# Norms of a state-space mixer: squares as the stationary operand, sums with time on the partitions

## The reference, cut to what matters

```python
proj = einsum('btd,od->bto', x, W_in)           # gate, value, and 2 step parameters a head
value = silu(conv(value_raw))
dt = clip(softplus(params[..., 0] + dt_bias), DT_MIN, DT_MAX)
kd = K_MAX * sigmoid(params[..., 1])
bc = einsum('bti,oi->bto', value, W_bc).reshape(Bsz, Tlen, H, 4, N)      # N = 32 states
bc = bc / (sqrt(sum(bc * bc, axis=-1, keepdims=True)) + EPS)             # the norms
Bz, Bx, Cz, Cx = bc[..., 0, :], bc[..., 1, :], bc[..., 2, :], bc[..., 3, :]
# a scan over time of two coupled states a head, driven by Bz * u and Bx * u, read by Cz and Cx
```

## Time and profile before

| what | value |
|---|---|
| median of 3 runs | 2361.71 us |
| the profiled execution | 2356.95 us |
| its span, first to last instruction | 2355.2 us |
| PE busy / DVE busy / ACT busy, share of the span | 86% / 87% / 46% |
| mix stage, 400 to 1990 us: PE / DVE busy | 1503.49 / 1505.45 of 1590 us |
| TensorE's granted clock, mean over the span | 0.947 |
| L681 (sums of squares), 512 passes | 267.9 us busy |
| DMA, mean over the span | 127 GB/s |

### The profile page before, as it was taken

How to read it: one execution, slowest core, us unless ns; L and a number is a source line. 1 busy time by engine, 2 the same in 40 slices (tenths; PEclk the granted TensorE clock), 3 DMA queues, 4 the chain that set the end, 5 groups by cost and what they waited for, 6 DMA issues and landing times. The chain is left out here.

```text
span 2355.2 us, 78715 instructions
## 1 busy us (share of the span) xinstructions
PE 2026.4 (86%) x31266; PEld 1059.6 (45%) x31266; DVE 2053.6 (87%) x5467; ACT 1080.7 (46%) x1700; POOL 83.4 (4%) x28
## 2 busy tenths in 40 slices
PE   6777469999999999899999999998999998357886
PEld 2333124444444444444444544444444444246675
DVE  6887589998999999999989999998999996487774
ACT  4665225544454444445444544444554544024453
POOL 0000000000000000000000000000000000153300
PEclk9898779999999999999999999999999999578997
DMA  4455644565555465545655554655456443443300
GB/s 137 176 212 177 177 93 105 130 143 130 128 129 129 121 142 128 123 106 133 143 128 130 126 128 112 146 132 123 105 131 145 108 97 85 149 160 134 143 27 27
DMA packets 224664, 300.27 MB, mean 127 GB/s; under 512 B 96784, under 2 KB 114192, under 8 KB 218128
## 3 DMA queue, kind: packets, MB, share of 16 engines
q1 hardware_dynamic: 174416, 212.11, 35.8%
q10 hardware_dynamic: 48704, 78.68, 12.9%
q0 software_dynamic: 1152, 4.19, 0.5%
HBM read 240.85 MB, written 50.86 MB: 124 GB/s over the span
## 5 line engine op out<-in xcount | busy, mean ns | idle before, releaser
L670 PE MATMUL m_ps_a<-m_valT,m_w_bc 128*128 128x512 f32 x2048 | 967.1, 611 | 50.4 <-DMA m_valT<-scratch_valT 33.8
L670 PEld LDWEIGHTS m_ps_a<-m_valT,m_w_bc 128*128 128x128 f32 x2048 | 366.8, 191 | 510.0 <-issue 503.6
L822 ACT ACTIVATE m_sq<-m_ps_a 128x512 f32<-128x512 f32 x256 | 152.9, 597 | 540.5 <-PE m_ps_a L670 536.8
L962 DVE TENSOR_TENSOR m_prod<-m_psi,m_shear 128x128 f32<-128x128 f32 x960 | 368.4, 384 | 0.0
L966 DVE TENSOR_TENSOR m_psi<-m_psi,m_prod 128x128 f32<-128x128 f32 x960 | 367.9, 383 | 0.0
L681 PE MATMUL m_ps_s<-m_sq,m_head_sum 128*32 128x512 f32 x512 | 267.9, 606 | 24.4 <-ACT m_sq L822 24.4
L693 PE MATMUL m_ps_g<-m_q,m_k 32*64 32x64 f32 x8192 | 124.8, 234 | 45.0 <-issue 37.2
L693 PEld LDWEIGHTS m_ps_g<-m_q,m_k 32*64 32x64 f32 x8192 | 108.9, 135 | 101.0 <-ACT m_dX L844 55.4
L823 ACT ACTIVATE m_raw<-m_ps_a 128x512 f32<-128x512 f32 x256 | 151.9, 593 | 0.0
L221 PE MATMUL ps_w<-p_xnT,w_in 128*128 128x512 f32 x256 | 119.4, 620 | 16.5 <-ACT gate L284 16.3
L756 PEld LDWEIGHTS m_ps_y<-m_q,m_X 32*16 32x16 f32 x7168 | 103.8, 93 | 53.3 <-issue 53.3
(11 more groups left out here) (143 smaller groups left out, 3085.4 us busy)
## 6 DMA issues: line engine op xcount, KB each, us to landing
m_scale<-scratch_norm SPq DMA_DIRECT2D x256, 256.0 KB, 5.3
m_w_bc<-in_w_bcT ACTq DMA_DIRECT2D x252, 256.0 KB, 3.8
m_shear<-scratch_n_alpha SPq DMA_DIRECT2D x64, 256.0 KB, 5.2
m_shear<-scratch_beta SPq DMA_DIRECT2D x256, 64.0 KB, 3.7
m_det<-scratch_gd SPq DMA_DIRECT2D x256, 64.0 KB, 4.5
scratch_gateT<-gate SPq DMA_DIRECT2D x8, 1024.0 KB, 3.9
scratch_valT<-val SPq DMA_DIRECT2D x8, 1024.0 KB, 4.5
scratch_svgT<-svg SPq DMA_DIRECT2D x8, 1024.0 KB, 5.8
```

The source lines that it names most:

```text
L670: mm = pe.matmul(ps_a[j % 2].ap(), w_bc[:, j, kt, :], valT[:, kt, :], start=(kt == 0), stop=(kt == KI - 1), skip_group_check=True)
L822: act.activation(sq[:, j % 2, :], ps_a[j % 2].ap(), ACT.Square).then_inc(sq_ready.sem, sq_ready.step)
L962: dve.tensor_tensor(prod.ap(), psi_t[half][:, :, :, :, t], shear_t[half][:, :, :, t].unsqueeze(1).to_broadcast([P, 2, 2, HALF * NC]), ALU. ...
```

## The change

In `mix` the sums of squares change sides. A quarter of `sq` (128 states by 128 times) becomes the stationary operand and 4 columns of `head_sum` the moving one, so a sum is four matmuls of 4 columns in place of one of 512 columns, and its result has time on the partitions: `ps_norm` [128, head, j, quarter]. ACT takes the root of [128, 64] into `norm`; DVE adds, inverts and multiplies `norm` in place. One transpose on PE (`transpose_rows`) turns [128, 64] into [64, 128] in another part of the same PSUM bank, ACT copies it out (`copy_rows`), and SP stores and spreads it as before. The four gathering DMAs and the three factor DMAs a unit go. `scales` of the next unit moves ahead of the operation that makes `q`.

In `project` PE turns `beta`, `dt` and `e_inv` at a row's end by three transposes into `ps_l`, ACT copies them as one tile `fac` [128, 384], and SP stores that in place of `dt` and `e_inv`; `mix` loads it once a row. The next row's logits, which also go to `ps_l`, wait for that copy.

```diff
+                    sp.wait_ge(fac_ready.sem, fac_ready.at(b, 0))
+                    sp.dma_start(dram["factor"][b], fac.ap()).then_inc(fac_stored.sem, fac_stored.step)
...
-                    pe.wait_ge(logit_ready.sem, logit_ready.at(b, -1))
+                    pe.wait_ge(fac_ready.sem, fac_ready.at(b, -1))
...
+                    pe.wait_ge(steps_ready.sem, steps_ready.at(b, 0))
+                    pe.wait_ge(logit_ready.sem, logit_ready.at(b, 0))
+                    for n, v in enumerate((beta, dt, e_inv)):
+                        mm = pe.transpose(ps_l[:, n * P:(n + 1) * P], v.ap(), ident.ap())
+                    mm.then_inc(fac_made.sem, fac_made.step)
...
+                    act.wait_ge(fac_made.sem, fac_made.at(b, 0))
+                    act.wait_ge(fac_stored.sem, fac_stored.at(b, -1))
+                    act.activation(fac.ap(), ps_l[:, 0:3 * P], ACT.Copy).then_inc(fac_ready.sem, fac_ready.step)
...
+        ps_norm = ps_s[:, 0:SEG].rearrange("p (h j c) -> p h j c", c=TT, j=NJ)
+        ps_rows = ps_s[0:SEG, P:2 * P]
...
-                def load_factor(b, group):
-                    for j, name in enumerate(("beta", "dt", "e_inv")):
-                        src = dram[name][b, group * HP:(group + 1) * HP, :].rearrange("h (s t) -> (h s) t", t=SEG)
-                        sp.dma_start(factor[j * N:(j + 1) * N, :], src).then_inc(factor_in.sem, factor_in.step)
-                def compact_norms(b, group):
-                    sp.wait_ge(norm_ready.sem, norm_ready.at(b, group))
-                    for j in range(NJ):
-                        sp.dma_start(compact[j * N:(j + 1) * N, :],
-                                     rows_[j * N:j * N + HP, :].rearrange("h (s t) -> h s t", t=SEG)
-                                     ).then_inc(compact_in.sem, compact_in.step)
+                def load_factor(b):
+                    sp.dma_start(factor.ap().rearrange("p j h c -> p (j h c)"), dram["factor"][b]
+                                 ).then_inc(factor_in.sem, factor_in.step)
                 def spread_scales(b, group, u_):
-                    sp.wait_ge(rows_ready.sem, rows_ready.at(b, group))
-                    sp.dma_start(dram["norm"][u_].rearrange("r (s t) -> (r s) t", t=SEG),
-                                 compact.ap()).then_inc(rows_stored.sem, rows_stored.step)
+                    sp.wait_ge(rows_copied.sem, rows_copied.at(b, group))
+                    sp.dma_start(dram["norm"][u_], rows_.ap()).then_inc(rows_stored.sem, rows_stored.step)
                     sp.wait_ge(rows_stored.sem, rows_stored.at(b, group))
                     sp.sem_inc(sp_passed, 1)
                     sp.wait_ge(scaled.sem, scaled.at(b, group - 1))
                     for h in range(HP):
-                        src = dram["norm"][u_].rearrange("(j h) t -> h j t", h=HP)[h]
+                        src = dram["norm"][u_].rearrange("(h j c) t -> h j (c t)", j=NJ, h=HP)[h]
...
-                    pe.wait_ge(norm_ready.sem, norm_ready.at(b, group - 1))
-                    pe.matmul(ps_s[j * N:(j + 1) * N, :], head_sum.ap(), sq[:, j % 2, :],
-                              start=True, stop=True, skip_group_check=True).then_inc(sums_made.sem, sums_made.step)
+                    pe.wait_ge(rows_copied.sem, rows_copied.at(b, group - 1))
+                    for c in range(TT):
+                        mm = pe.matmul(ps_norm[:, :, j, c], sq[:, j % 2, c * P:(c + 1) * P], head_sum[:, 0:HP],
+                                       start=True, stop=True, skip_group_check=True)
+                    mm.then_inc(sums_made.sem, sums_made.step)
+                def transpose_rows(b, group):
+                    pe.wait_ge(rows_ready.sem, rows_ready.at(b, group))
+                    pe.sem_inc(passed, 1)
+                    pe.transpose(ps_rows, norm.ap().rearrange("p h j c -> p (h j c)"), ident.ap()
+                                 ).then_inc(rows_made.sem, rows_made.step)
...
-                def inner(b, group, ahead):
+                def inner(b, group, more, ahead):
                     s = group % 2
                     if ahead:
                         product(b, group + 2, 0, (0, 1, 2))
+                    if more:
+                        transpose_rows(b, group + 1)
...
+                    if group == 0:
+                        transpose_rows(0, 0)
...
-                    act.wait_ge(compact_in.sem, compact_in.at(b, group * NJ - 1))
-                    act.activation(rows_.ap(), ps_s.ap(), ACT.Sqrt).then_inc(norm_ready.sem, norm_ready.step)
+                    act.wait_ge(rows_made.sem, rows_made.at(b, group - 1))
+                    act.activation(norm.ap(), ps_norm, ACT.Sqrt).then_inc(norm_ready.sem, norm_ready.step)
+                def copy_rows(b, group):
+                    act.wait_ge(rows_made.sem, rows_made.at(b, group))
+                    act.wait_ge(rows_stored.sem, rows_stored.at(b, group - 1))
+                    act.activation(rows_.ap(), ps_rows, ACT.Copy).then_inc(rows_copied.sem, rows_copied.step)
...
                         store_y(b, group)
+                        if more:
+                            copy_rows(b, group + 2)
                         if here:
                             copy_dX(b, unit)
...
-                    dve.wait_ge(compact_in.sem, compact_in.at(b, (group + 1) * NJ - 1))
-                    dve.tensor_scalar(compact.ap(), compact.ap(), NORM_EPS, None, ALU.add).then_inc(own.sem, own.one())
+                    dve.wait_ge(norm_ready.sem, norm_ready.at(b, group))
+                    dve.tensor_scalar(norm.ap(), norm.ap(), NORM_EPS, None, ALU.add).then_inc(own.sem, own.one())
                     between(1)
                     dve.wait_ge(own.sem, own.n)
-                    dve.reciprocal(compact.ap(), compact.ap()).then_inc(own.sem, own.one())
+                    dve.reciprocal(norm.ap(), norm.ap()).then_inc(own.sem, own.one())
                     between(1)
-                    dve.wait_ge(factor_in.sem, factor_in.at(b, 3 * (group + 1) - 1))
-                    dve.wait_ge(own.sem, own.n)
-                    dve.tensor_tensor(compact.ap(), compact.ap(), factor.ap(), ALU.mult).then_inc(rows_ready.sem, rows_ready.step)
+                    heads = slice(group % HG * HP, (group % HG + 1) * HP)
+                    dve.wait_ge(factor_in.sem, factor_in.at(b, group // HG))
+                    dve.wait_ge(own.sem, own.n)
+                    dve.tensor_tensor(norm[:, :, 0:NJ - 1, :], norm[:, :, 0:NJ - 1, :],
+                                      factor[:, :, heads, :].rearrange("p j h c -> p h j c"),
+                                      ALU.mult).then_inc(rows_ready.sem, rows_ready.step)
...
                                           psi[:, :, 1, group, :, 1:], ALU.mult).then_inc(own.sem, own.one())
                         advance(1)
+                        if not (last and group == LAST):
+                            scales(b, group + 1, advance)
                         dve.tensor_tensor(by_chunk(q[s])[:, ::-1], over_rows_of(r4[:, 3, :]),
...
-                        if not (last and group == LAST):
-                            scales(b, group + 1, advance)
                         dve.wait_ge(y_made.sem, y_made.at(b, group - 1))
```

59 lines of the change are left out of this document (32 added, 27 removed).

## The result

The changed kernel takes 2376.27 us (median of 20 runs, 2364.24 to 2395.08), the kernel before 2357.63 (20 runs, 2347.77 to 2366.44). The ratio is 1.0082, with a 95% interval of 1.0064 to 1.0101: slower by 0.8%, where 1.1% less time was forecast (2336 against the 2361.71 then known). The profiled execution took 2378.26 us, its span is 2376.6; before they were 2356.95 and 2355.2.

The account below looks back on a forecast made before the run. PE was taken to lead the mix stage, DVE following with 1.1 us to spare. From 2356.95: 0.57 us a group over 62, less 3, gains 32; -4.5 +4 +7 gives 2331.5, forecast 2336 us; 8-in-10 range 2312 to 2385.

Parts of the forecast that it names:

- Otherwise the stage ran at 1.00: Mix stage before the change: granted clock at 1.00 except at a turn of a row, where it fell to 0.57.
- the fall of the clock: Rival, mix stage: mostly-loading sums 3 and 4 drop PE's clock, 1.7 us a fall; a third of groups 2370 us; chance 0.18.
- a sign of error: Listed signs include PEclk below 0.97 between 400 and 1990 us, or project longer by more than 14 us.
- The sums: PE, mix: 0.88 us a sum in place of 1.17, passes 0.11 apart; gains 0.29 twice, 0.27, 0: 0.85 a group.
- The turn of the norms: PE, mix: one transpose with a change of shape costs 0.28 us a group; its wait for DVE's scales is covered.
- pace kept by `dX` and VectorE: Rival, mix: copy, transpose and instruction waits eat the 0.57 us a group; 2368 us, or 2357 with a third; chance 0.20.
- 1 us for each of 7 rows: Project: next row's logits wait for transposes and ACT's copy; 1.9 us worked out, 1 taken, 7 us lost in all.
- First group: Mix stage's start: the shorter root lets DVE go on earlier than with the gathered norms; 4.5 us gained.
- The end: Mix stage's end: the norms' store comes 1 to 2 us later in the last three groups; 4 us lost.
- The 3 us for instructions: PE, mix: some 50 more instructions a group, waited for in denser stretches; 3 us taken off the gain.
- waits longer for `k`: PE, mix: `k` was ready at 1026.35, before PE's transposes at 1026.86; no cost was counted for this wait.
- The rule that the prediction weighed against the change: Loads run beside matmuls only when the row group differs; a pass would take at least 0.19 us and the change lose.

Follow-up runs that it names:

- e2: Changed kernel with only sums 3 and 4 of a group moving 256 columns a pass in place of 4: 2418.86 us, 1.0259 of the kernel before.
- e3: Changed kernel with only sums 1 and 2 of a group moving 256 columns a pass in place of 4: 2435.08 us, 1.0317 of the kernel before.
- e4: Changed kernel with project's factor transposes, copy and store placed behind the next row's logits and other work: 2361.95 us, 1.0018 of the kernel before.
- e5: Changed kernel with all four sums moving 128 columns a pass in place of 4: 2368.63 us, 1.0037 of the kernel before.
- e6: Changed kernel with project's factors turned late and all sums moving 128 columns a pass: 2346.47 us, 0.9955 of the kernel before.
- e8: Changed kernel with project's factors turned late and all sums moving 64 columns a pass: 2349.03 us, 0.9955 of the kernel before.
- e11: Changed kernel with factors turned late, a quarter of the next product ahead of the further outputs, sums at 64 columns: 2346.22 us, 0.9949 of the kernel before.
- e1: Changed kernel with all four sums moving 256 columns a pass in place of 4: 2512.28 us, 1.0646 of the kernel before.

## Why the prediction was wrong, point by point

- **That failed: "Otherwise the stage ran at 1.00", carried into the sum as a full clock.** The forecast gave the fall of the clock 0.18 and said that the trace does not show whether loads hold it. They don't hold it here: PEclk 0.96, below the 0.97 that it named as a sign of error, 28 stretches, 20 of them with TensorE busy up to the fall, 33 to 50 us by the two regressions. e2 and e3 show the cause and the place. The rival's size was close: 1.7 us for each fall in a third of the groups, 2370 us; measured are 1.2 to 1.8 us a stretch.
- **The sums were right.** Loads follow each other at 0.11 us (seven in 0.86), product and sum take 4.35 us (4.3 forecast). Forecast 0.85 a group, measured 0.61 (0.52 + 0.10 - 0.01): the third sum gained 0.10 of the 0.27, the rest is nearly right. The turn of the norms costs 0.11 in place of 0.28 and never waits. Net 0.50 of 0.57.
- **Rival "pace kept by `dX` and VectorE"** is not the main cause, but it is not excluded either. Groups without a fall take 26.14 us, as the forecast's 26.1, but they are mostly those at the short places of a row; with a mean for each place the level without falls is 26.7 us, before 26.85, and in e4, with the same code in the mix stage, 26.8. So most of the 0.50 us that TensorE's starts show does not arrive in the groups by this measure.
- **Mis-sized: project, "1 us for each of 7 rows".** The forecast worked out 1.9 us for a row and took 1, because a part would be hidden. Nothing was: a row takes 1.90 us more in the mean, 13.3 in seven. The start of the logits was nearly right (1.2 to 1.6 us behind `gd`, 1.1 worked out), but the clock had no part in the forecast: it stays down over the waits, and the seven rows' logits take 3.0 to 3.7 us, before 1.9 to 2.5. 2.1 us more come at the stage's end, where the last factors are turned and stored with nothing beside them, and 1.6 up to the first product. e4 took it away by place alone. 17 us is over the 14 named as a sign of error.
- **First group:** -4.3 for -4.5. **The end:** the 4 us lost did not come. **The 3 us for instructions:** TensorE's waits by "issue" between 400 and 1990 us fell, from 75.7 to 69.8 us over all lines.
- Put together: the groups are 43 us off the forecast, 27 to 37 by the clock (33 less the 6 of before, or 50 less 13) and 4 by the sums (0.07 in 62 groups). The other 2 to 12 us stay open; the 8 us by which TensorE waits longer for `k` are of that size, and the forecast put this wait at nothing. 2331.5 + 43 for the groups + 10 for project - 4 for the end - 2.4 for the last stage is 2378, the profiled execution.

One rule of the Trainium skill was missing from the forecast's weighing. "TensorE: Matmul & The Clock Gate", Part 1, "HAM oscillation — how this bites in real kernels", has the clock fall where TensorE stands idle between bursts, waiting for data. The trace agrees in kind, with shorter waits than in the page's example: in the projection the clock is at 0.50 behind a wait of 2.83 us, and 8 of the mix stage's 28 falls have a wait of 1.2 us or more ahead. The mix stage goes beyond the rule: at 1017 us, and 19 times more, the clock fell with no idle time ahead of it. The rule that the prediction weighed against the change, Part 3, "What overlaps and what doesn't" of the same page of the Trainium skill, is contradicted once more, by e5: its seven loads take the same 0.86 us although every pass between them moves 128 columns.

**What stays open:** whether any order of these sums at four columns holds the clock without a new wait. Three orders were tried, none did. Open too is how the groups' loss divides between the clock and longer waits, beyond the bounds above. The best versions measured, e6, e8 and e11, win 0.45 to 0.5% over the kernel before, none of it in the groups: some 6 us up to the first product and 4 in the first group.

## What to carry to other kernels

A matmul with the data as stationary operand and a handful of moving columns is priced by its load, but ask as well what the clock does: put its neighbours together, see whether a stretch is left in which TensorE mostly loads, and price the unchanged work behind that stretch at both clock levels. More moving columns held the clock here, but cost about what they won. A wait that a change puts ahead of TensorE can cost twice, once as the wait and once as the half-speed work behind it; placing the dependent step behind work that is already there cost nothing here. And before a regression prices a clock, compare groups of the same place in the loop.

## What the runs showed that I had not expected

- A busy TensorE can lose its clock. With 94% busy in both kernels, PEclk was 1.00 before and 0.96 after. Stretches that begin with no idle time of TensorE ahead, by the columns that a pass of sums 3 and 4 moves: with 4 columns 20 (the changed kernel, and again e4) and 18 (e3); with 64, 128 or 256 columns none in seven runs (e1, e2, e5 to e8, e11).
- Load and stream of an fp32 pass overlap: passes on 128x128 blocks follow each other at 0.11 us with 4, 64 or 128 columns, at 0.22 us with 256 and 0.43 us with 512.
- Unchanged work shows the clock best: the outputs' mean of 214 ns went to 237 and came back to 214.
